# Two buffers per part of q and k in the projection, and a later load of the second stack

## What is computed

```python
q = split_heads(x @ Wq + bq)
k = split_heads(x @ Wk + bk)
v = split_heads(x @ Wv + bv)
scores = jnp.einsum('bhqd,bhkd->bhqk', q, k) / jnp.sqrt(jnp.float32(dk))
scores = jnp.where(causal[None, None], scores, -jnp.inf)
attn = jax.nn.softmax(scores, axis=-1)
out = jnp.einsum('bhqk,bhkd->bhqd', attn, v)
```

## Time and profile before

| what | value |
|---|---|
| median of 3 runs | 894.93 us (894.47 to 896.44) |
| the profiled execution's own time | 893.04 us |
| its span, first to last instruction | 891.3 us |
| TensorE busy, share of the span | 818.8 us, 92% |
| VectorE busy | 643.1 us, 72% |
| ScalarE busy | 484.3 us, 54% |
| GpSimd busy | 341.4 us, 38% |
| mean granted clock of TensorE | 0.967 |

### The profile page before, as it was taken

How to read it: one execution, slowest core, us unless ns; L and a number is a source line. 1 busy time by engine, 2 the same in 40 slices (tenths; PEclk the granted TensorE clock), 3 DMA queues, 4 the chain that set the end, 5 groups by cost and what they waited for, 6 DMA issues and landing times. The chain is left out here.

```text
span 891.3 us, 17342 instructions
## 1 busy us (share of the span) xinstructions
PE 818.8 (92%) x5250; PEld 456.0 (51%) x5251; DVE 643.1 (72%) x1747; ACT 484.3 (54%) x728; POOL 341.4 (38%) x464
## 2 busy tenths in 40 slices
PE   7987999999999999999999999899996999999910
PEld 3554534434434343434443443389663888888810
DVE  6346899999999999999999996168775222227774
ACT  2443367667666766666666765656521344444443
POOL 5442412111221122111211122276477777655583
PEclk9999999999999999999999999999898899999965
DMA  8698363587556644685235500136133666567855
GB/s 275 211 251 190 124 91 41 105 144 105 90 109 108 97 63 107 120 145 71 37 39 72 74 1 4 50 124 204 43 108 106 211 185 187 174 183 233 273 181 207
DMA packets 90442, 114.60 MB, mean 129 GB/s; under 512 B 9232, under 2 KB 70928, under 8 KB 90384
## 3 DMA queue, kind: packets, MB, share of 16 engines
q1 hardware_dynamic: 74176, 85.22, 45.0%
q0 software_dynamic: 7680, 21.11, 6.5%
q10 hardware_dynamic: 8528, 7.50, 2.6%
HBM read 62.74 MB, written 50.66 MB: 127 GB/s over the span
## 5 line engine op out<-in xcount | busy, mean ns | idle before, releaser
L734 ACT ACTIVATE work<-ps 128x1024 f32<-128x1024 f32 (+3 forms) x384 | 293.8, 809 | 154.3 <-PE ps L805 151.9
L689 POOL TENSOR_SCALAR_AFFINE_SELECT work<-work 128x512 f32<-128x512 f32 x128 | 81.2, 634 | 371.7 <-ACT work L734 371.7
L358 DVE TENSOR_REDUCE m_neg<-ps 128x1 f32<-128x512 f32 (+2 forms) x304 | 195.1, 684 | 8.3 <-PE ps L334 5.3
L354 DVE CUSTOM_DVE_ANT_0 ps<-ps,wgu 128x384 f32<-128x384 f32 (+1 forms) x256 | 154.3, 649 | 15.2 <-PE ps L334 14.8
L334 PE MATMUL ps<-stacks 96*128 96x512 bf16 (+3 forms) x528 | 144.7, 329 | 8.0 <-DVE m_neg L354 4.6
L805 PE MATMUL ps<-stacks 99*128 99x512 bf16 (+3 forms) x528 | 125.4, 326 | 2.2 <-ACT work L734 1.7
L820 PE MATMUL ps<-work,vg 128*32 128x512 f32 (+3 forms) x1056 | 110.8, 497 | 0.4 <-POOL work L689 0.2
L1091 POOL DMA_INDIRECT z_back<-v_home,home x96 | 92.3, 962 | 47.5 <-ACT v_home L1165 27.4
L334 PEld LDWEIGHTS ps<-stacks 96*128 96x128 bf16 x528 | 49.2, 97 | 100.6 <-DVE m_neg L358 33.0
L1485 PE MATMUL ps<-wgu,work 128*128 x384 | 92.0, 383 | 0.0
L1333 DVE TENSOR_TENSOR work<-work,ps 128x256 f32<-128x256 f32 x48 | 20.2, 422 | 93.1 <-ACT work L1159 93.1
(11 more groups left out here) (142 smaller groups left out, 1156.0 us busy)
## 6 DMA issues: line engine op xcount, KB each, us to landing
stacks<-qk_parts SPq DMA_DIRECT2D x132, 128.0 KB, 6.8
work<-y_sorted SPq DMA_DIRECT2D x48, 260.0 KB
qk_parts<-work SPq DMA_DIRECT2D x32, 384.0 KB, 5.1
y_sorted<-wgu SPq DMA_DIRECT2D x7, 1560.0 KB, 7.9
work<-z_back SPq DMA_DIRECT2D x32, 256.0 KB, 3.8
wgu<-qk_parts SPq DMA_DIRECT2D x60, 128.0 KB, 6.2
work<-in_xT SPq DMA_DIRECT2D x8, 512.0 KB, 4.3
work<-in_x SPq DMA_DIRECT2D x8, 512.0 KB, 4.0
```

The lines of the kernel that those rows point to most:

```text
L354: dve.tensor_tensor_reduce(out=scores, in0=scores, in1=wide_mask[:, CH - w:], scale=-1.0, scalar=-NEG, op0=ALU.add, op1=ALU.min, accum_out ...
L358: dve.tensor_reduce(dst, ps[:, bank, 0:heads * w].rearrange("p (h k) -> p h k", h=heads), AX.X, ALU.max, negate=True).then_inc(reduced, 1)
L689: pool.affine_select(out=blk_, in_=blk_, compare_op=ALU.is_ge, fill=0.0, base=0, pattern=[[0, GH], [1, P]], channel_multiplier=-1).then_in ...
L734: act.activation(probs[:, s + 2 * pair:s + 2 * pair + 2, off:CH], ps[:, SCORE_BANK + 2 * pair:SCORE_BANK + 2 * pair + 2, off:CH], ACT.Exp, ...
```

## The change

`parts` becomes two sets of four: chunks with an even number use the old words in `work`, those with an odd number words of `a_all`. `stored` becomes two sets of four semaphores. `high` of chunk c waits for the store of chunk c - 2 in place of c - 1. Since nothing else then holds `rest[t]` back, VectorE's L574 gets a wait for the low part of the chunk before. Stack 1 is loaded along with the stores of chunk 5 in place of chunk 4. In step 0 ScalarE's unit 2 waits only for the stores of even chunks, and VectorE waits for the stores of odd chunks before its first instruction of the step.

```diff
-            parts = [piece(4096 + 768 * t, 768).bitcast(BF16).rearrange("p (r t) -> p r t", r=3) for t in range(4)]
+            a_words = a_all[:, :, :, :].rearrange("p a b c -> p (a b c)")
+            parts = [[words.bitcast(BF16).rearrange("p (r t) -> p r t", r=3) for words in of] for of in
+                     ([piece(4096 + 768 * t, 768) for t in range(4)],
+                      [a_words[:, 768 * t:768 * t + 768] for t in range(4)])]
...
-            stored = [sem(f"stored{t}") for t in range(4)]
+            stored = [[sem(f"stored{k}_{t}") for t in range(4)] for k in range(2)]
...
                     if stack is not None:
                         for t in range(4):
-                            sp.wait_ge(stored[t], 16 * HALVES)
+                            for k in range(HALVES):
+                                sp.wait_ge(stored[k][t], 16)
...
-                            .rearrange("r p t -> p r t"), parts[t]).then_inc(stored[t], 16)
+                            .rearrange("r p t -> p r t"), parts[c % 2][t]).then_inc(stored[c % 2][t], 16)
...
-                    store(c, {2: 0, 4: 1}.get(c))
+                    store(c, {2: 0, 5: 1}.get(c))
...
-                def high(c, t):
+                def high(c, b, half, t):
                     act.wait_ge(proj_ready[t], c + 1)
-                    wait_count(act, stored[t], 16 * c)
-                    act.activation(parts[t][:, 0, :], ps[:, t, :], ACT.Identity,
+                    wait_count(act, stored[half][t], 16 * b)
+                    act.activation(parts[half][t][:, 0, :], ps[:, t, :], ACT.Identity,
...
                         dve.wait_ge(hi_ready, c * 4 + t + 1)
+                        wait_count(dve, lo_ready, c * 4 + t - 3)
...
-                            act.wait_ge(stored[t], 16 * CHUNKS)
+                            act.wait_ge(stored[0][t], 16 * B)
...
+                for t in range(4):
+                    dve.wait_ge(stored[1][t], 16 * B)
                 step(0, first=True)
```

More of the change, by code:

```diff
@@ L504, in low @@
                         pool.wait_ge(mid_ready, c * 4 + t + 1)
-                        pool.tensor_tensor(parts[t][:, 2, :], rest[t], parts[t][:, 1, :],
+                        pool.tensor_tensor(parts[half][t][:, 2, :], rest[t], parts[half][t][:, 1, :],
                                            ALU.subtract).then_inc(lo_ready, 1)
@@ L528, in project_scalar, with middle @@
                 act.wait_ge(bqk_loaded, 32)
-                def high(c, t):
+                def high(c, b, half, t):
                     act.wait_ge(proj_ready[t], c + 1)
-                    wait_count(act, stored[t], 16 * c)
-                    act.activation(parts[t][:, 0, :], ps[:, t, :], ACT.Identity,
+                    wait_count(act, stored[half][t], 16 * b)
+                    act.activation(parts[half][t][:, 0, :], ps[:, t, :], ACT.Identity,
                                    bias=bqk[:, t // 2, t % 2:t % 2 + 1]).then_inc(hi_ready, 1)
-                def middle(c, t):
+                def middle(c, half, t):
                     act.wait_ge(rest_ready[t], c + 1)
-                    act.activation(parts[t][:, 1, :], rest[t], ACT.Copy).then_inc(mid_ready, 1)
+                    act.activation(parts[half][t][:, 1, :], rest[t], ACT.Copy).then_inc(mid_ready, 1)
                 def split(c, b, half):
-                    high(c, 0)
+                    high(c, b, half, 0)
                     for t in range(1, 4):
-                        high(c, t)
-                        middle(c, t - 1)
-                    middle(c, 3)
+                        high(c, b, half, t)
+                        middle(c, half, t - 1)
+                    middle(c, half, 3)
                 staggered(act, [(0, split)], CHUNKS)
@@ L573, in take @@
                         dve.wait_ge(hi_ready, c * 4 + t + 1)
+                        wait_count(dve, lo_ready, c * 4 + t - 3)
                         dve.scalar_tensor_tensor(rest[t], ps[:, t, :], bqk[:, t // 2, t % 2:t % 2 + 1],
-                                                 parts[t][:, 0, :], ALU.add, ALU.subtract)\
+                                                 parts[half][t][:, 0, :], ALU.add, ALU.subtract)\
                             .then_inc(rest_ready[t], 1)
@@ L665, in _ @@
                 step(0, 0)
-                for t in range(4):
-                    sp.wait_ge(stored[t], 16 * CHUNKS)
+                for k in range(HALVES):
+                    for t in range(4):
+                        sp.wait_ge(stored[k][t], 16 * B)
                 sp.wait_ge(blank_ready, 2)
@@ L702, in clear_third @@
                     for t in (2, 3):
-                        pool.wait_ge(stored[t], 16 * CHUNKS)
+                        pool.wait_ge(stored[0][t], 16 * B)
                     pool.memset(vg[2][:, :, :, DK:32], 1.0).then_inc(ones_ready, 1)
```

## The result

The changed kernel takes 886.35 us, the median of 4 runs (885.22 to 889.86), against 895.68 us for the kernel before in the same comparison (4 runs, 894.47 to 896.79). The ratio is 0.9904, with a 95% interval from 0.9881 to 0.9928: 9.3 us faster. The changed kernel run again gave 885.99 us, ratio 0.9887 (0.9868 to 0.9905). Forecast were 885.0 us and 9.95 us.

A forecast was written before the change was run, and what follows sets the result against it. Bound: late stores behind stack loads in one queue stall ScalarE, VectorE, then TensorE in chunks 4 and 5. 2.60 + 7.35 = 9.95 us, other terms 0; 894.93 - 9.95 = 885.0 us, range 883.0 to 889.5 us.

The forecast's parts named there:

- The reading of the bound: Projection: ScalarE's 36.3 us of store waits cost nothing by themselves; they hold VectorE, then TensorE, in chunks 4 and 5.
- Chunk 4: Projection chunk 4: stores of chunk 2 land in time, so it takes chunk 3's 10.32 us, saving 2.60 us.
- Chunk 5: Projection chunk 5: priced at the mean of chunks 6 and 7, 14.27 us, saving 7.35 us, clock loss included.
- Chunk 6: Projection chunk 6: no saving or loss in the sum; its profiled 14.86 us served to price chunk 5.
- Stack 1 later at no cost: Loads moved to chunk 5's stores land by about 85 us, needed at about 104: hidden by some 19 us.
- The wait ahead of step 0: VectorE's wait for chunk 7's last store, landing after 2.5 us, ends 0.2 us before anyone would notice: cost 0.
- VectorE's twelve waits for the low part: Chunks 5 to 7: at most 0.5 us, taken as 0 because VectorE has idle time there.
- A: Rival, chance 0.12: the DMA queue still holds chunk 5, half its excess stays, 3.7 us come back: 888.7 us.
- B: Rival, chance 0.08: VectorE's new wait before step 0 costs 2.4 us at the median store landing: 887.4 us.
- C: Rival, chance 0.03: slower, 896.1 us, if stack loads take twice their time, past 9.9 us of slack behind stack 1.
- its own last sign: If the attention starts at 102 us and the end is not 10 us earlier, the forecast is wrong behind the projection.

The follow-up runs named there:

- before's repeat: The kernel before, run again with no edit for a second profile: 895.6 us, ratio 1.0007.
- the added loads: The changed kernel with extra stack loads behind chunk 2's stores: twelve 895.13 us, ratio 1.0002 to the kernel before; four 886.85 us, ratio 0.9892.
- VectorE's wait later: The changed kernel with VectorE's wait for odd chunks' stores moved from step 0's start to just ahead of the attention result's first write: 885.34 us, ratio 0.9878.
- twelve loads in chunk 5: The changed kernel with 12 extra stack loads behind chunk 5's stores and stack 1: 885.43 us, ratio 0.9893 to the kernel before.

## Why the prediction was right, step by step

**The reading of the bound** was right. The 36.3 us of ScalarE's waits were worth about 9 us: in chunks 1 to 3 they vanished too, and each of those takes 10.32 us in both kernels.

**Chunk 4**, 2.60 us: measured 12.92 - 10.32 = 2.60 us against before's first profile, the one that the forecast used. In before's repeat the chunk takes 14.22 us, and the same 10.32 us would be a gain of 3.90.

**Chunk 5**, 7.35 us: measured 21.62 - 14.31 = 7.31 us. Pricing it by its kin was good, and the added loads reproduce the mechanism in the other direction, clock included. That it came within 0.04 us is luck: the two kin lie more than 1 us apart, with the 15.19 us that chunk 6 takes in nearly every profile their mean is 14.4 us, and against before's repeat the gain is 20.88 - 14.31 = 6.57 us. One working step was off without harm: chunk 3's four stores were to be issued within 1.5 us and were spread over 3.88.

**Chunk 6** was taken to stay at 14.86 us, and that is the term that was missed: it takes 15.19 us, 0.33 us more. In before's repeat it takes 15.18 us too, and in the kernel with the later stack alone 15.19, so 14.86 was the exception of one profile and not the rule. Together with chunk 0, which took until 18.32 us in place of 18.00, this gives the attention's start: 2.60 + 7.31 - 0.33 - 0.32 = 9.26 us, which is 112.04 - 102.78. Chunk 0 ends between 17.57 and 18.59 us in the ten profiles, in no order with the edits: spread.

**Stack 1 later at no cost**: right, and more than that. It has no benefit either beside the second buffers. The prediction said where the loads are hidden and did not ask what they are worth alone; alone they bring 5 us.

**The wait ahead of step 0**, taken as 0, measured 0.40 us at L372 and 0.23 us in the attention's length. The last store was issued at 101.95 us and L372 started 3.06 us later, against 2.70 before. The four stores of chunk 7 landed after a median of 2.6 us, but the last one, for which L372 waits, took 2.8:

```profile
qk_parts<-a_all SPq DMA_DIRECT2D x1, 384.0 KB, 2.8
```

That is 104.75 us, 0.14 us behind the end of the last reduction (104.61), so the 0.2 us of slack was used up. The term was put at nothing on a landing of 2.5 us, and the store took 2.8 us in the changed kernel, in its repeat, with only the second buffers and with VectorE's wait later. The Trainium skill's fixed cost (DMA: Bandwidth & Descriptors, Anatomy of one DMA), an estimated landing of 2.9 us, would have made this term 0.2 us. The page fits that cost on DMAs issued from GpSimd, and this store is issued by SyncE; the trace's 2.8 us agrees with the estimate to 0.1 us all the same. Why the last store takes 2.8 us there and 2.5 before is open. So is a part of the effect: with twelve loads in chunk 5 the last store took 2.5 us, L372 had no DMA as its releaser and stood 0.14 us behind the last reduction, against 0.04 before, and the attention still took 459.27 us (102.03 to 561.30).

**VectorE's twelve waits for the low part**, taken as 0: chunk 7 takes 13.68 us with and without them.

**The rivals.** A did not happen, but the slack is real and small: 0.9 to 3.6 us of queue, gone with twelve more loads and, in the execution profiled, with four. The Trainium skill says (Trainium Kernel Development and Optimization, Key Constraints) that DMAs issued from SyncE, ScalarE and GpSimd all run on the same 16 DMA engines. Here SyncE's queue alone holds them at a share of 1.08 in chunks 4 and 5; several issuing engines were not tried. That a buffer adds no bandwidth is the prediction's own step from there, and the share bears it out: it was at its full value before too. B happened in a tenth of its price. C's slack behind stack 1 was tested by 12 loads and held. Its other half was not thought of: work ahead of chunk 3's stores has little slack, and there 12 loads take back all of the gain.

**Behind the projection** the profiles lose 2.8 us, 9.26 against 6.44 us for the execution. By its own last sign the prediction would have been called wrong behind the projection. Before's repeat shows that the stretch after the attention differs by 4.3 us between executions of one program, and the medians (9.3 us) agree with the attention's start. The sign compared one profile with one profile, and that was too little.

## What to carry to other kernels

A wait is worth what the bound engine loses by it: compare a stretch with its kin that do the same work, and take the kin's length as the price, with the clock that a gap costs already in it. Before a buffer is added, look at what delays the transfer that frees it; here moving twelve loads gave half the gain for one changed digit. After it is added, ask how long before its next need each store lands, store by store and not on the average, and ask it of more than one profile.

## What was not expected of the hardware

The time from issue to landing behind the same queue differs by up to 2.7 us between executions: 8.0 to 10.7 us for the first store of chunk 3 in the five profiles with two buffers and nothing added ahead of it.

The price of a stack load in a full queue was put at 0.9 us from the whole stretch. Counted from the start of chunk 4, the store landed 6.2 to 8.9 us later with four more loads of 128 KB than in those five profiles, which is 1.5 to 2.2 us for each, and 11.7 to 14.4 us later with twelve more, which is 1.0 to 1.2 us for each. Both are single executions, the one with four loads the slowest of its six. Whether the price of a load varies or the whole queue was slower in that execution is open.
